# Two transformer layers on one core: where queries travel and in which order the last steps run

## The reference, cut

```python
# x: 32 sequences of 64 tokens, 512 features; cond: 32 x 512
# layer 0: 8 query heads of 64, one key/value head
h = ada_rms(x, cond)                         # x*rsqrt(mean x^2)*w*(1 + cond @ tw.T)
q, k, v = heads(h @ Wq.T), heads(h @ Wk.T), heads(h @ Wv.T)
q, k = apply_rope(q), apply_rope(k)
x = x + softmax(q @ k.T / 8) @ v @ Wo.T
h = ada_rms(x, cond)
x = x + (silu(h @ Wg.T) * (h @ Wu.T)) @ Wd.T   # 512 -> 2048 -> 512
# layer 1: 16 query heads of 32, 4 key/value heads through a latent of 128
h = layernorm(x) * (1 + scale(cond)) + shift(cond)
q, c = h @ Wq.T, h @ Wkd.T
k, v = c @ Wku.T, c @ Wvu.T
out = x + softmax(rope(q) @ rope(k).T / sqrt(32)) @ v @ Wo.T
```

## Time and profile before

| | us |
|---|---|
| median of 3 runs (854.05 to 855.15) | 854.21 |
| the profiled execution | 856.11 |
| its span, on which all rows stand | 854.3 |
| PE busy | 832.0 (97%) |
| DVE busy | 604.1 (71%) |
| ACT busy | 417.3 (49%) |
| POOL busy | 398.4 (47%) |

### The profile page before, as it was taken

How to read it: one execution, slowest core, us unless ns; L and a number is a source line. 1 busy time by engine, 2 the same in 40 slices (tenths; PEclk the granted TensorE clock), 3 DMA queues, 4 the chain that set the end, 5 groups by cost and what they waited for, 6 DMA issues and landing times.

```text
span 854.3 us, 15030 instructions
## 1 busy us (share of the span) xinstructions
PE 832.0 (97%) x5688; PEld 680.7 (80%) x5688; DVE 604.1 (71%) x877; ACT 417.3 (49%) x729; POOL 398.4 (47%) x311
## 2 busy tenths in 40 slices
PE   8899999999999999999999999999999999999897
PEld 5688788788788788787888877887887888887775
DVE  6788466666665666766557788876866867868986
ACT  4555445345345345345347456355364373445552
POOL 1566545545544545446457555455354444422220
PEclk9999999999999999999999999999999999999999
DMA  9902533533533533523533445436345255130001
GB/s 341 370 26 75 166 115 114 177 116 102 179 103 101 179 110 106 179 83 119 180 132 122 155 162 177 153 128 192 105 160 188 83 175 171 58 106 25 14 26 38
DMA packets 73335, 113.50 MB, mean 133 GB/s; under 512 B 6320, under 2 KB 39088, under 8 KB 73264
## 3 DMA queue, kind: packets, MB, share of 16 engines
q1 hardware_dynamic: 72544, 112.45, 39.1%
q10 hardware_dynamic: 720, 0.09, 0.1%
HBM read 88.15 MB, written 24.38 MB: 132 GB/s over the span
## 4 chain that ended last, share of the span: by engine, by line
PE 78%; DVE 6%; issue 5%; DMA 4%; POOL 3%; ACT 3%; SPq 0%; ACTq 0%; DVEq 0%; POOLq 0%
PE ps L696 25%; PE ps L698 24%; PE ps L697 24%; DVE ex L1447 2%; PE ps L789 1%; PE ps L741 1%; PE ps L973 1%; DMA pT<-turned_p 1%; DMA turned_q<-tq 1%; PE ps L820 1%; POOL wol L621 1%; PE ps L998 1%; ACT yf L1869 1%; POOL yl L596 1%; DMA turned_y<-txy 1%
## 5 line engine op out<-in xcount | busy, mean ns | idle before, releaser
L696 PE MATMUL ps<-h2h,guh 128*128 128x512 f32 x512 | 203.6, 398 | 0.0
L698 PE MATMUL ps<-h2l,guh 128*128 128x512 f32 x512 | 200.1, 391 | 0.0
L697 PE MATMUL ps<-h2h,gul 128*128 128x512 f32 x512 | 199.7, 390 | 0.0
L559 POOL TENSOR_TENSOR gul<-rgu,guh 128x1024 fp32r<-128x1024 f32 x64 | 161.1, 2518 | 73.6 <-ACT guh L1777 73.6
L564 POOL TENSOR_TENSOR wdl<-rwd,wdh 128x512 fp32r<-128x512 f32 x64 | 82.9, 1296 | 131.1 <-ACT wdh L1785 131.1
L1339 DVE TENSOR_TENSOR xres<-ps,xres 128x512 f32<-128x512 f32 x128 | 87.5, 684 | 63.5 <-PE ps L698 62.8
L696 PEld LDWEIGHTS ps<-h2h,guh 128*128 128x128 f32 x512 | 96.1, 188 | 27.6 <-issue 7.5
L698 PEld LDWEIGHTS ps<-h2l,guh 128*128 128x128 f32 x512 | 96.2, 188 | 20.9
L697 PEld LDWEIGHTS ps<-h2h,gul 128*128 128x128 f32 x512 | 96.3, 188 | 19.1
L696 PE MATMUL ps<-wdh,ah 128*128 128x512 f32 x256 | 100.1, 391 | 0.0
L697 PE MATMUL ps<-wdh,al 128*128 128x512 f32 x256 | 99.8, 390 | 0.0
(11 more groups left out here) (179 smaller groups left out, 1580.5 us busy)
## 6 DMA issues: line engine op xcount, KB each, us to landing
rgu<-gu SPq DMA_DIRECT2D x64, 512.0 KB, 4.6
rwd<-WdT SPq DMA_DIRECT2D x64, 256.0 KB, 4.2
turned_q<-tq SPq DMA_DIRECT2D x20, 320.0 KB, 2.6
qkT<-turned_q SPq DMA_DIRECT2D x20, 320.0 KB, 3.1
turned_p<-tp SPq DMA_DIRECT2D x9, 512.0 KB, 2.6
pT<-turned_p SPq DMA_DIRECT2D x9, 512.0 KB, 3.9
xt<-xT SPq DMA_DIRECT2D x16, 256.0 KB, 3.8
out<-xres SPq DMA_DIRECT2D x15, 256.0 KB, 3.5
```

Source lines behind the costliest of these rows:

```text
L559: pool.tensor_tensor(gul[i][:, :], rgu[i][:, :], guh[i][:, :], ALU.subtract).then_inc(m_gul, 1)
L696: pe.matmul(dst, lh, rh, start=start, stop=False)
L697: pe.matmul(dst, ll, rh, start=False, stop=False)
L698: return pe.matmul(dst, lh, rl, start=False, stop=stop)
```

## The change

1. **Head's norm in a bank of the scores.** `x2_bank(t)` is `XB[3]` for tiles 0 to 2, instead of `BU`; `x2_T` waits for `a_ch`, `a_cl` only for tile 3; `context(t)` in the head no longer waits for `a_gf` of the tile before, and `scores(t)` for t = 3, 4, 5 waits for `a_gf` of t-2 instead. ACT copies the next tile's queries in the head right after the probabilities.
2. **Queries' store and load on ACT's queue.** The four functions are moved from SP's program into ACT's. In layer 0 the store stands after `f1` and two pieces of `f2`, the load after `high_h(s+2)`; in layer 1 the store after `f3`, the load after `high_y(u+2)`.
3. **The last steps.** `context1(u)` stands in step u itself, ahead of the next scores; `p_T1` comes before `qk_T1`; `probs_T1` is divided between ACT (first bank, `b_pTa`) and DVE (second bank, `b_pTb`); `high_ctx1` and `low_ctx1` move to the same step; POOL adds the keys' rope halves for all tiles (DVE's L1413 and `b_kr` are gone); `stats1(u+3)` comes right behind `softmax_scale1`, ahead of `add_out`.

```diff
@@ x2_bank, and in scores, context, x2_T (PE)
-            return BU
+            return XB[3] if t < HEAD - 1 else BU
...
+                if 2 < t <= HEAD + 1:
+                    pe.wait_ge(a_gf, t - 2)
...
-                    wait(pe, a_gf, t - 1)
...
-                pe.wait_ge(a_ch, t + 2)
-                pe.wait_ge(a_cl, t + 2)
+                if t == HEAD - 1:
+                    pe.wait_ge(a_ch, t + 2)
+                    pe.wait_ge(a_cl, t + 2)
@@ rope_sum1 (POOL) and rope_mul1 (DVE)
-                if t <= TAIL:
-                    pool.tensor_tensor(halves(qkr1[:, D:D + P]), part(u1, 8, 10), part(u2, 8, 10), ALU.add)
+                pool.tensor_tensor(halves(qkr1[:, D:D + P]), part(u1, 8, 10), part(u2, 8, 10), ALU.add)
...
-                    dve.tensor_tensor(qkr1[:, D:D + P].rearrange("p (c n) -> p c n", c=2), keys(u1), keys(u2),
-                                      ALU.add).then_inc(b_kr, 1)
@@ layer 1's loop on PE
-                if TAIL < u < NT:
-                    context1(u - 1)
...
+                if TAIL < u < NT - 1:
+                    p_T1(u)
                 fill(pieces, f3)
                 if u >= TAIL and in_layer(u + 1):
                     qk_T1(u + 1)
-                if TAIL < u < NT - 1:
-                    p_T1(u)
-                if 0 <= u < TAIL:
+                if 0 <= u < NT - 1:
                     context1(u)
@@ layer 1's loop on DVE
-                if u > TAIL:
-                    low_ctx1(u - 1)
...
                 if u > TAIL and in_layer(u):
                     softmax_scale1(u)
+                if u > TAIL and in_layer(u + 3):
+                    stats1(u + 3)
...
+                if u > TAIL:
+                    probs_T1(u)
                 fill(pieces, f3)
+                if u > TAIL and in_layer(u + 3):
+                    mean_rstd(u + 3)
                 if u >= TAIL and in_layer(u + 1):
                     keys1(u + 1)
-                if u > TAIL and in_layer(u + 3):
-                    stats1(u + 3)
-                    mean_rstd(u + 3)
-                if 0 <= u < TAIL:
+                if in_layer(u):
                     low_ctx1(u)
@@ ACT: the four functions (sp. becomes act.) and their places
+            def queries_back(t):
+                n = t - TURN_Q0
+                act.wait_ge(st_q0, 16 * (n + 1))
+                act.wait_ge(a_sc, t)
+                back(qkT, dq0[t, :, :], ld_q0)
...
-                fill(pieces, f2)
+                fill(pieces, min(f2, 2))
+                if TURN_Q0 <= s + 1 < NT:
+                    queries_away(s + 1)
+                fill(pieces, f2 - min(f2, 2))
...
                 if s == NT - 2:
                     high_w1_queries()
+                if TURN_Q0 <= s + 1 < NT:
+                    queries_back(s + 1)
...
+                if u < TAIL:
+                    queries_away1(u + 1)
...
                     scale_shift_y(u + 2)
                     high_y(u + 2)
+                    queries_back1(u + 1)
```

More of the change, by code:

```diff
@@ L193, in build @@
         (b_bn, b_mv, b_var, b_rstd, b_nb, b_xn, b_xT, b_yf, b_hh, b_hl, b_qkv, b_rope, b_qks,
-         b_v, b_kr, b_qkT, b_qka, b_qkb, b_sc, b_max, b_ds, b_ex,
-         b_sum, b_rec, b_p, b_pTr, b_pT, b_ctx, b_ch, b_cl, b_wo, b_out, b_st) = [
+         b_v, b_qkT, b_qka, b_qkb, b_sc, b_max, b_ds, b_ex,
+         b_sum, b_rec, b_p, b_pTr, b_pTa, b_pTb, b_ctx, b_ch, b_cl, b_wo, b_out, b_st) = [
             sem("b_" + n) for n in (
-            "bn mv var rstd nb xn xT yf hh hl qkv rope qks v kr qkT qka qkb sc "
-            "max ds ex sum rec p pTr pT ctx ch cl wo out st").split()]
+            "bn mv var rstd nb xn xT yf hh hl qkv rope qks v qkT qka qkb sc "
+            "max ds ex sum rec p pTr pTa pTb ctx ch cl wo out st").split()]
         def bank(k):
@@ L383, in y_back @@
                 back(yt, dy[t, :, :], ld_yT)
[L385 to L395, removed]
             def probs_away1(t):
@@ L1025, in context_last @@
                 t = NT - 1
-                pe.wait_ge(b_pT, 2 * (t - TAIL) + h + 1)
-                pe.wait_ge(b_v, t + 1)
+                if h == 0:
+                    pe.wait_ge(b_pTa, t - TAIL + 1)
+                    pe.wait_ge(b_v, t + 1)
+                else:
+                    pe.wait_ge(b_pTb, t - TAIL + 1)
                 pe.wait_ge(b_ds, 2 * NT)
@@ L1479, in keys1, with probs_T1 @@
                                     from_bank).then_inc(b_qkb, 1)
+            def probs_T1(t):
+                dve.wait_ge(b_pTr, t - TAIL + 1)
+                wait(dve, b_ctx, t)
+                dve.tensor_copy(words(pT1[:, :, KT:2 * KT, :]), in_words(by_feature(bank(banks1(t)[3])))
+                                ).then_inc(b_pTb, 1)
             def low_ctx1(t):
@@ L1823, in _, with away, back, queries_away @@
             pieces = mlp()
+            def away(tile, to, cols, signal):
+                act.dma_start(to, tile[:, 0:cols]).then_inc(signal, 16)
+            def back(tile, turn, signal):
+                act.dma_start(tile[:, :, :, :].rearrange("p w k f -> p w (k f)"),
+                             turn.rearrange("(w f) (q c) -> (f q) w c", w=W, q=W)).then_inc(signal, 16)
+            def queries_away(t):
+                n = t - TURN_Q0
+                act.wait_ge(a_tq, n + 1)
+                away(tq, dq0[t, :, :], D + P, st_q0)
+            def queries_back(t):
+                n = t - TURN_Q0
+                act.wait_ge(st_q0, 16 * (n + 1))
+                act.wait_ge(a_sc, t)
+                back(qkT, dq0[t, :, :], ld_q0)
+            def queries_away1(t):
+                act.wait_ge(b_tq, t + 1)
+                away(tq, dq1[t, :, :], D + P, st_q1)
+            def queries_back1(t):
+                act.wait_ge(st_q1, 16 * (t + 1))
+                if t == 0:
+                    act.wait_ge(a_rope, NT)
+                    act.wait_ge(a_sc, NT)
+                wait(act, b_sc, t)
+                back(qkT1, dq1[t, :, :], ld_q1)
             def high_w1_queries():
@@ L1902, in probs_T1 @@
             def probs_T1(t):
+                act.wait_ge(b_pTr, t - TAIL + 1)
                 wait(act, b_ctx, t)
-                for h in range(2):
-                    act.wait_ge(b_pTr, 2 * (t - TAIL) + h + 1)
-                    act.copy(words(pT1[:, :, KT * h:KT * (h + 1), :]), in_words(by_feature(bank(banks1(t)[2 + h])))
-                             ).then_inc(b_pT, 1)
+                act.copy(words(pT1[:, :, 0:KT, :]), in_words(by_feature(bank(banks1(t)[2])))).then_inc(b_pTa, 1)
             def high_ctx1(t):
@@ L1914, in probs_T_last @@
             def probs_T_last(h):
[L1915 removed]
+                act.wait_ge(b_pTr, NT - TAIL + h)
                 if h == 0:
@@ L1918, in probs_T_last @@
                 act.copy(words(pT1[:, :, h::2, :]), in_words(by_feature(bank(banks1(NT - 1)[2 + h])))
-                         ).then_inc(b_pT, 1)
+                         ).then_inc(b_pTb if h else b_pTa, 1)
             def high_ctx_last(h):
```

48 lines of the change are left out of this document (11 added, 37 removed).

## The result

The changed kernel takes 887.26 us (median of 4 runs, 885.02 to 891.25) beside 854.57 for the kernel before in the same comparison: ratio 1.039, 95% interval 1.036 to 1.042. It is 33 us slower. The forecast was 857.5 with a range to 862.0: the direction was right, the size wrong by a factor of ten. The medians are 32.7 apart: this execution (885.02 us) was the shortest of the four, and the one profiled for the kernel before (856.11) was longer than its four runs.

What follows compares the result with a forecast made beforehand. TensorE, busy 97% of 854.3 us, was taken to bound the kernel, so new stalls count in full. Queries' transfers +8.4, last steps −5.0, head −0.1 gave +3.3 on 854.2: 857.5 us, range 851.8 to 862.0.

Steps and rivals of the forecast that it cites:

- Part 1, the tight loads: Layer 0, every second tile's queries' load on ScalarE's queue: five stalls of 1.2 us, 6.0 in all (0.3 to 9.5).
- such a load takes 2.9, 3.1 or 3.6 us: Least, median and most time from issue to landing of a `qkT` load, used to size the stalls.
- Part 1, layer 1: Layer 1's queries' loads behind `high_y`: 1.4 us more at step 0, 0.5 in each step beside it, others 0.
- Step 0: Layer 1's first step: load lands 1.1 to 2.4 us beyond today's 1.44 wait, so PE waits 2.5 to 3.5.
- The others are longer: 0: Layer 1's remaining steps have more time from `high_y` to the scores: no stall, up to 2 us together.
- my sentence that ScalarE is not held by its wait for the store: ScalarE's instructions behind the load are held no longer than today's by the transfer; the store's wait should be over.
- Part 2, the last steps: Layer 1's last steps: period 11.25 us instead of 12.50, plus gains at entry and end; −5.0 us (−6.5 to −1).
- rival C: Last steps: GpSimd gets the shared port first, product takes 2.32 us, only the end is won; 861.6 us, chance 0.12.
- Part 3, the head: Head: PE's `qkT` waits go, but `h2l` still bounds the MLP's start; −0.1 us (−1.1 to 0.3).
- B: Load issued early enough, landing by 138.2: stalls about 2 us in all, 851.1 us, faster; chance 0.20.
- D: Cancel: stalls of 3.5 to 6.8 us are given back by the last steps, within 0.2%; chance 0.22.
- A: The forecast itself: tight steps stall 1.2 us, last steps win 5, +3.3; stalls 7 to 12 give 856 to 861.4; chance 0.46.

## Why the prediction was wrong in size

**Part 1, the tight loads: the moment was right, the landing mis-sized.** I took the load to be issued somewhere between the moment when `high_h`'s operand is ready and the end of `high_h`; it goes out at 201.52, 0.1 us behind the operand (DVE's `xt` ends at 201.42) and ahead of `high_h`'s start at 202.01, so at the early bound. The step that failed is "such a load takes 2.9, 3.1 or 3.6 us". Those were landings of loads that SyncE issued ahead of its next weights, in layer 0 some 11 us ahead of need (192.04, the next weights at 192.46). At the new moment the same load has 768 KB of weights ahead of it and takes 4.0 to 7.1 us in the five tight steps. I had even read a weight load of 5.1 us beside it and used it only to round 1.2 upward. 6.0 expected, 11.6 measured, with an upper end of 9.5. The first tight wait, 1.21, equals my 1.2 by luck: the load went out earlier than the moment I had in mind and took 4.00 us instead of 3.1.

**Part 1, layer 1.** 2.4 expected, 13.7 − 1.4 = 12.3 measured. Step 0 was right: the wait is 2.97 (2.5 to 3.5 forecast). The tiles on either side of it, 0 and 2, wait 1.91 and 1.07 where I had put 0.5 each, and tiles 3 to 8 wait 7.8 in all. "The others are longer: 0" is the sentence that fell, for two reasons. In the even tiles the load goes out at `high_y`, as I had it, but behind the weights, and takes 4.0 to 6.2 us. In tiles 1, 3, 5 and 7 it goes out when the store has landed, which took 6.1 to 7.5 us. I had looked at `high_y` and not at the store, which had moved behind `f3`. ScalarE's rows for tile 3:

```profile
575.58 0.33 ACTq L1799 DMA_DIRECT2D turned_q<-tq  x1
...
582.46 0.38 ACTq L1803 DMA_DIRECT2D qkT<-turned_q  x1
...
582.94 0.60 ACT L1762 ACTIVATE sg<-ps 128x512 f32<-128x512 f32 x1 [0.76 <-DMA turned_q<-tq]
```

The store lands at 582.44, and the load follows at once. Before, too, the stores of layer 1 took long (4.3 to 6.8 us but for the first) and each load went out as its store landed; it then landed only 0.4 to 3.2 us ahead of the scores in tiles 2 to 9. In tiles 3, 5 and 7 the store now goes out 1.0 to 1.1 us later against the scores and takes 0.8 to 1.4 us longer, which is more than the room of 1.0 to 1.5 there. The last row also answers my sentence that ScalarE is not held by its wait for the store: it is, for 3.7 us in three of the steps.

**What I left out: the clock.** 9.5 us. I counted a stall as its own length. In the middle of this kernel four of the five waits of layer 0 and one of layer 1 are followed by a stretch at 0.92 to 0.95 of the granted clock, 1.25 to 1.6 us dearer in layer 0's steps (33.75 against 32.50 in the first) and 2.7 in layer 1's (36.16 against 33.48). The trace of before could have warned of it, since its end shows 0.61 behind waits.

**Part 2, the last steps: right.** One of them after, as it answers to the earlier trace rows (DVE's product, GpSimd's two sums, then two successive starts of the scores):

```profile
818.07 1.22 DVE L1412 TENSOR_TENSOR ex<-ex,smx 128x1024 f32<-128x1024 f32 x1
...
818.23 1.37 POOL L577 TENSOR_TENSOR qkr<-u 128x128 f32<-128x128 f32 x1 [6.50 <-DVE u L1378]
...
819.56 1.27 POOL L578 TENSOR_TENSOR qkr<-u 128x512 f32<-128x512 f32 x1
...
822.33 0.91 PE L944 MATMUL ps<-qkT 32*64 32x64 f32 x64
...
833.52 0.91 PE L944 MATMUL ps<-qkT 32*64 32x64 f32 x64
```

The period is 11.16 to 11.21 (11.25 forecast). The product takes 1.22 us, GpSimd's sum of the keys, 0.46 alone, takes 1.37 because it waits for the port, and ends 0.3 us behind the product: DVE was first, as forecast, and rival C did not occur. By the rule of the Trainium skill ("SBUF — State Buffer", section "Who interferes with whom") the one that issues first has the port for its whole instruction; the trace agrees, 818.07 against 818.23. From the scores of tile 9 to the end it is 883.1 − 794.15 = 88.95 us, against 854.3 − 760.75 = 93.55: 4.6 won, 5.0 forecast. The steps gave 4.0 of it (3.7 + 0.4 forecast), the end 0.6 (1.35 forecast): from the last tile's first maximum to the transpose of its second half it is 6.06 us, not 5.25.

```profile
868.36 0.68 DVE L1467 TENSOR_REDUCE smx<-ps 128x8 f32<-128x512 f32 x1
...
874.42 0.66 PE L991 MATMUL ps<-idn,ex 128*128 128x128 f32 x4
```

**Part 3, the head:** −0.1 forecast, 0.03 seen in the trace.

Sum with the measured terms: 23.9 of added idle time, 9.5 of clock, −4.6 at the end: 28.8, the difference of the two spans.

Of the rivals, B had the moment right (the sequencer hands the load out as soon as the operand is there) and the landing wrong: that of tile 7 comes at 139.22, not by 138.2. D falls by the sum of the stalls, 23.9 against 3.5 to 6.8, and C by the product's 1.22. None of them was what came. Small slips of the prediction change nothing: by its own terms A's upper figure is 861.1 and not 861.4, and the range starts at 851.8, above B's own 851.1. And the steps of 12.50 us with a wait for `yl` were three, as the sum had it, and not all of the last ones. The range's upper end added up longest landings of loads ahead of the weights and was cut to 14 "since not every transfer is the longest"; the true sum, 23.9, lay above even the uncut 18.

## What to carry to other kernels

Before a transfer is moved, look at what else is in flight at its new moment and in what order the queues will send it: a landing time holds for its own neighbourhood only. Here a late load ahead of the bulk loads in one queue made TensorE wait at most 0.36 us; on the other queue nothing kept the bulk loads behind it, and it waited up to 3.58. Look also at whether the transfer can go out at all at its place: four loads of layer 1 hung on the landing of their store. And in this kernel, where TensorE is busy for 97%, most stalls of 2 to 4 us cost more than their length.

## What the runs showed that I had not expected

One and the same load, issued 2.9 us ahead of need on the same queue, makes PE wait 0.36 us with 768 KB of weights behind it and 2.58 with them ahead (853.4 against 868.9 us for the kernels). And the end of the kernel varies with the clock; the last 8 us of the kernel after, and of the version with the queries on SyncE:

```profile
875.00:883.10 8.10, 4.87 (x41) 4.21 (x40) 1.69 (x4) 0.96 (x2) 0.00 (x0) 0.79 0.18 65
```

```profile
840.00:847.80 7.80, 4.53 (x60) 3.69 (x60) 2.46 (x6) 1.33 (x3) 0.00 (x0) 1.00 0.19 67
```

The granted clock is 0.79 and 1.00 there. The runs of this version spread likewise: over the whole execution the granted clock is 1.000 where it takes 849.65 us and 0.994 where it takes 854.59; at which place it fell in the slower ones no trace shows. The best version measured is that one, the change without part 2: 850.78 us.
